# Joining three stages of an eight-layer transformer kernel: attention 1, routed feed forward 1 and retention

## The reference

```python
x = x + _L1_xattn_ref(_layernorm(x), ctx_1024, ctx_1024, mask, bias, ...)   # 16 heads of 8
x = x + _L1_ffn_ref(_layernorm(x), ...)
x = x + _L2_xattn_ref(_layernorm(x), ctx_1024, ctx_1024)                    # retention

# _L1_ffn_ref: 8 experts of inner width 64, 2 chosen, and a shared one of 128
logits = xf @ gate_w.T + lb_bias
scores = jax.nn.sigmoid(logits)
topw, topi = jax.lax.top_k(scores, K)
topw = topw / (topw.sum(-1, keepdims=True) + 1e-08)
for e in range(E):
    m = topi == e
    sel = m.any(axis=-1)
    wmean = (topw * m).sum() / jnp.maximum(m.sum(), 1)
    y = _mlp(xf, expert_gate_w[e], expert_up_w[e], expert_down_w[e])
    out = out + jnp.where(sel[:, None], y * wmean, 0)
out = out + _mlp(x, shared_gate_w, shared_up_w, shared_down_w)

# retention: q = xpos(Q), k = xpos(K): rotations of pairs; scores under a decay mask
scores = jnp.einsum('bhsd,bhtd->bhst', q, k) * D[None]
out = jnp.einsum('bhst,bhtd->bhsd', scores, v)
```

## Time and profile before

| | |
|---|---|
| median of 3 runs | 1600.39 us (1596.59 to 1604.29) |
| the profiled execution's own time | 1595.35 us, span 1593.5 us |
| TensorE, VectorE, ScalarE, GpSimd busy | 87%, 63%, 56%, 49% of the span |
| attention 1 | about 760 to 1006.35 us of the span |
| norm, gate and operands of feed forward 1 | 1006.4 to 1039.8 us |
| feed forward 1 | 1039.8 to 1099.8 us |
| norm and first rotation of retention | 1099.8 to 1120.35 us |
| retention | 1120.35 to 1180.8 us |
| feed forward 2, matmuls | about 1215 to 1311.9 us |

### The profile page before, as it was taken

How to read it: one execution, slowest core, us unless ns; L and a number is a source line. 1 busy time by engine, 2 the same in 40 slices (tenths; PEclk the granted TensorE clock), 3 DMA queues, 4 the chain that set the end, 5 groups by cost and what they waited for, 6 DMA issues and landing times.

```text
span 1593.5 us, 37007 instructions
## 1 busy us (share of the span) xinstructions
PE 1389.0 (87%) x14394; PEld 853.0 (54%) x14394; DVE 1006.3 (63%) x2452; ACT 887.8 (56%) x1456; POOL 774.9 (49%) x703
## 2 busy tenths in 40 slices
PE   5999999987899999998899898485776987999948
PEld 3666666655677777776344343243553553444425
DVE  5877777795634444447688888645664334666653
ACT  4877777765689999997444443121332223555512
POOL 5877777774579999897423231202301004334200
PEclk9999999998899999999799999698787996999968
DMA  8000000000112100010010110000000000000000
GB/s 260 8 8 2 8 8 8 2 15 28 31 32 90 56 26 26 26 47 28 4 60 31 38 50 1 1 0 27 2 3 1 1 7 4 8 8 5 1 1 27
DMA packets 26078, 39.53 MB, mean 25 GB/s; under 512 B 7060, under 2 KB 13112, under 8 KB 25432
## 3 DMA queue, kind: packets, MB, share of 16 engines
q1 hardware_dynamic: 25368, 35.58, 7.0%
q0 software_dynamic: 576, 2.10, 0.7%
HBM read 38.72 MB, written 1.05 MB: 25 GB/s over the span
## 4 chain that ended last, share of the span: by engine, by line
PE 67%; DVE 22%; issue 4%; ACT 4%; POOL 2%; DMA 1%; SPq 0%; POOLq 0%; DVEq 0%; ACTq 0%
PE bank L1660 10%; PE bank L1601 9%; PE bank L1927 5%; PE bank L681 5%; DVE sbuf L810 4%; PE bank L1913 4%; PE bank L1100 3%; PE bank L619 3%; DVE sbuf L827 2%; PE bank L1169 2%; PE bank L635 2%; DVE sbuf L332 2%; PE bank L1150 2%; PE bank L1120 2%; PE bank L1917 2%
## 5 line engine op out<-in xcount | busy, mean ns | idle before, releaser
L1611 ACT ACTIVATE sbuf<-bank,sbuf 128x512 f32<-128x512 f32 (+1 forms) x512 | 323.0, 684 | 36.7 <-PE bank L1601 24.7
L1631 POOL TENSOR_TENSOR sbuf<-sbuf 128x512 f16<-128x512 f32 x256 | 304.3, 1196 | 61.1 <-ACT sbuf L1611 59.9
L1660 PEld LDWEIGHTS bank<-sbuf 128*128 128x128 f16 x3072 | 194.9, 99 | 73.5 <-issue 14.5
L1660 PE MATMUL bank<-sbuf 128*128 128x128 f16 x3072 | 215.4, 220 | 12.4 <-DVEq L1748 6.3
L1601 PE MATMUL bank<-sbuf 128*128 128x512 f16 x768 | 209.1, 382 | 0.1
L810 DVE TENSOR_REDUCE sbuf<-bank 128x4 f32<-128x1024 f32 x128 | 156.2, 1221 | 75.6 <-PE bank L635 62.7
L312 POOL TENSOR_TENSOR sbuf<-sbuf 128x4 f32<-128x4 f32 (+2 forms) x21 | 28.3, 1349 | 348.1 <-DVE sbuf L307 348.1
L1063 POOL TENSOR_TENSOR sbuf<-sbuf 128x512 f16<-128x512 f32 x128 | 148.1, 1178 | 70.3 <-ACT sbuf L1279 70.2
L588 POOL TENSOR_TENSOR sbuf<-sbuf 128x512 f16<-128x512 f32 x64 | 66.6, 1040 | 234.9 <-ACT sbuf L740 234.9
L1743 DVE SCALAR_TENSOR_TENSOR sbuf<-bank,sbuf 128x128 f32<-128x128 f32 x256 | 71.7, 342 | 171.1 <-PE bank L1660 164.1
L681 PE MATMUL bank<-sbuf 128*32 128x256 f32 x2048 | 138.4, 389 | 1.6 <-ACT sbuf L760 1.6
(11 more groups left out here) (254 smaller groups left out, 2674.2 us busy)
## 6 DMA issues: line engine op xcount, KB each, us to landing
sbuf<-w SPq DMA_DIRECT2D x32, 256.0 KB, 2.9
sbuf<-bias_t SPq DMA_DIRECT2D x4, 1024.0 KB, 12.8
sbuf<-ctx_t SPq DMA_DIRECT2D x24, 128.0 KB, 3.5
sbuf<-bias_q POOLq DMA_DIRECT2D x4, 512.0 KB, 10.5
sbuf<-mask_t SPq DMA_DIRECT2D x8, 256.0 KB, 2.8
sbuf<-bias_t SPq DMA_DIRECT2D x8, 256.0 KB, 3.1
sbuf<-mask_q SPq DMA_DIRECT2D x8, 256.0 KB, 3.6
sbuf<-bias_q SPq DMA_DIRECT2D x8, 256.0 KB, 3.9
```

The costliest lines, as they stand in the source:

```text
L1611: last = act.activation(to, bank[u % 4][:, :], ACT.Gelu, bias=b1[u // U][:, u % FT0:u % FT0 + 1], scale=1 / SCALE)
L1631: g.tensor_tensor(hid16[1][:, u % BUFS, :], hid[:, u % 4, :], hid16[0][:, u % BUFS, :], ALU.subtract)\
L1660: last = pe.matmul(bank[4 + out_no % 2][:, j * P:(j + 1) * P], hid16[h][:, u % BUFS, j * P:(j + 1) * P], w2_16[p][:, w, f * D:(f + 1) * D] ...
```

## The change

`Gate` takes the place of `gate()` for feed forward 1 and works in two parts, tiles 0 to 11 and 12 to 15. `narrow_attention` gets two more arguments. Inside its loop VectorE takes the statistics of batch b-1 in unit 7 and scales batch b-2 in unit 1; GpSimd takes the power, splits the weights once (batch 1) and splits `xn_t` batch by batch; TensorE transposes batch b-2 in unit 2 and ScalarE copies it. In batch 7 the logits of the first part follow in unit 3 and their bias and negation in unit 4; after the loop come sigmoid, maxima and places of the first part between the last batch's steps.

`routed_feed_forward` takes the place of `feed_forward(1)`, unrolled. The four shared steps stand first, two of them before the gate; the projection down lags two steps. The mean goes into the fp16 spread table, whose high and low parts lie in different partitions (rows 0 to 7 and 32 to 39 of 64), so that one matmul makes the spread. Statistics and scaling of the next norm, the first two rotations of the queries (VectorE) and all rotations of keys (GpSimd) stand inside this stage; the context is loaded at its start, and retention's buffers lie apart from it. Feed forward 2 gets the same stacked spread. The diff, cut:

```diff
+        class Gate:
...
+            PARTS = ((0, 12), (12, TILES))
+            CHOSEN = 3
...
+            def logits(self, pe, h, to):
+                a, z = self.PARTS[h]
+                E = self.E
+                pe.wait_ge(nrm_xt, self.nm.ready(z // SB - 1))
+                for t in range(a, z):
+                    last = pe.matmul(to[:, (t - a) * E:(t - a + 1) * E], xn_t[:, t * P:(t + 1) * P], self.weights[:, 0:E],
+                                     start=True, stop=True)
+                last.then_inc(g_psum, 1)
...
+            def scores(self, v, h, src):
...
+            def exps(self, act, h):
...
+            def top(self, v, h):
...
+            def places(self, v, a, z):
...
+            def choose(self, v, h):
...
+            def turn(self, pe, k, to):
+                pe.wait_ge(g_ready, self.base["ready"] + (1 if k < self.CHOSEN else 2))
...
@@ -596,6 +725,17 @@
                 for b in range(B):
                     for k in range(QK):
                         split_(b, k)
+                    if after and b == 1:
+                        lead.weights(g)
+                    if after and b >= 2:
+                        after.power(g, b - 2, b - 1)
+                    if after and b >= 3:
+                        lead.halves(g, b - 3)
+                if after:
+                    lead.halves(g, B - 3)
+                    for b in (B - 2, B - 1):
+                        after.power(g, b, b + 1)
+                        lead.halves(g, b)
...
@@ -685,6 +825,8 @@
 
                 def out(b):
                     pe.wait_ge(s["normed"], b + 1)
+                    if after and b == B - 2:
+                        lead.gate.read(pe, 0)
...
+                    if after and b >= 2 and n == 2:
+                        after.turn(pe, b - 2, b - 1, bank[TR])
+                    if after and b >= 2 and n == 3:
+                        pe.wait_ge(nrm_xt, after.ready(b - 2))
...
+                    if after and b == B - 1 and n == 3:
+                        pe.wait_ge(x_done, x0 + B - 2)
+                        lead.gate.logits(pe, 0, bank[PR])
...
+                if after:
+                    after.turn(pe, B - 2, B - 1, bank[TR])
...
+                    if after and b >= 2 and n == 2:
+                        after.copy(act, b - 2, b - 1, bank[TR])
...
+                if after:
+                    lead.gate.exps(act, 0)
+                    after.copy(act, B - 2, B - 1, bank[TR])
...
+                    if after and b >= 2 and n == 1:
+                        after.scale(v, b - 2, b - 1)
                     if b and n == 2:
                         norm_out(b - 1)
                     if b and n == 6:
                         out(b - 1)
+                    if after and b and n == 7:
+                        v.wait_ge(x_done, x0 + b)
+                        after.stats(v, b - 1, b)
+                    if after and b == B - 1 and n == 4:
+                        lead.gate.scores(v, 0, bank[PR])
+                if after:
+                    after.scale(v, B - 2, B - 1)
+                    lead.gate.top(v, 0)
                 norm_out(B - 1)
+                if after:
+                    lead.gate.places(v, 0, 8)
                 out(B - 1)
+                if after:
+                    v.wait_ge(x_done, x0 + B)
+                    after.stats(v, B - 1, B)
+                    lead.gate.places(v, 8, 12)
+                    after.scale(v, B - 1, B)
...
+        def routed_feed_forward(layer, nm, after, ahead):
...
+            LAG = 2
+            RING = 4
...
+            inners = [(c, routed) for c in range(CHUNKS)] + [(c, t) for c in range(CHUNKS) for t in range(routed)]
+            downs = [(c, t) for c in range(CHUNKS) for t in [routed] + list(range(routed))]
...
+            def weights(g):
...
+            def halves(g, k):
...
+                def inner(m):
+                    c, t = inners[m]
+                    if m < CHUNKS:
+                        pe.wait_ge(s["x16"], 4 * c + 4)
+                    if m == 0:
+                        pe.wait_ge(s["w16"], WEIGHTS)
+                    if m >= 2:
+                        pe.wait_ge(s["hidden"], m - 1)
+                    if t < routed:
+                        gate.ready(pe, c)
+                        pe.wait_ge(s["spread"], 1)
...
+                    for b0, w16 in ((0, wg16), (2, wu16)):
+                        for k, (w, xk) in enumerate(PASSES):
+                            last = pe.matmul(bank[b0 + m % 2][:, :], w16[:, w, t * P:(t + 1) * P], x16[:, xk, cols],
+                                             start=k == 0, stop=k == 2)
+                    if t < routed:
+                        last = pe.matmul(bank[SPREADS[m % 2]][:, :], spread16[0:ROWS, t * P:(t + 1) * P],
+                                         gates16[0:ROWS, cols], start=True, stop=True)
+                    last.then_inc(s["inner"], 1)
...
+                for m in range(2):
+                    inner(m)
+                pe.wait_ge(nrm_xt, nm.ready(B - 2))
+                nm.turn(pe, B - 1, B, bank[TURNED])
+                gate.logits(pe, 1, bank[LOGITS])
+                for k in range(CHUNKS - 1):
+                    if k == 1:
+                        gate.read(pe, 1)
+                    if k >= 2:
+                        gate.ready(pe, k - 2)
+                    gate.turn(pe, k, bank[SPREADS[k % 2]])
+                gate.total(pe, bank[TOTALS])
+                gate.ready(pe, 1)
+                gate.turn(pe, CHUNKS - 1, bank[SPREADS[(CHUNKS - 1) % 2]])
+                for m in range(2, CHUNKS):
+                    inner(m)
+                d = 0
+                for m in range(CHUNKS, len(inners) + LAG):
+                    if m < len(inners):
+                        inner(m)
+                    while d < len(downs) and inner_no[downs[d]] <= m - LAG:
+                        down(d)
+                        d += 1
...
+                nm.copy(act, B - 1, B, bank[TURNED])
+                gate.exps(act, 1)
+                for k in range(CHUNKS):
+                    gate.turned(act, k)
+                    src = bank[SPREADS[k % 2]][0:E, :]
+                    cols = slice(k * CHUNK, (k + 1) * CHUNK)
+                    act.activation(gates16[HIGH, cols], src, ACT.Copy)
+                    act.activation(gates16[LOW, cols], src, ACT.Copy).then_inc(g_t, 1)
+                for m in range(len(inners)):
+                    act.wait_ge(s["inner"], m + 1)
+                    wait(act, s["hidden"], m - RING + 1)
+                    act.activation(acted[:, m % RING, :], bank[m % 2][:, :], ACT.Silu, scale=1 / SCALE).then_inc(s["acted"], 1)
...
+                def add(k):
+                    v.wait_ge(s["down"], (k + 1) * NT)
+                    xs = x[:, k * CT:(k + 1) * CT, :]
+                    v.tensor_tensor(xs, bank[DOWNS[k % 2]][:, :].rearrange("p (t d) -> p t d", d=D), xs, ALU.add)\
+                     .then_inc(x_done, 1)
+                    v.wait_ge(x_done, x0 + k + 1)
+                    after.stats(v, 2 * k, 2 * k + 2)
...
+                gate.choose(v, 0)
+                gate.scores(v, 1, bank[LOGITS])
+                gate.top(v, 1)
+                gate.places(v, 12, TILES)
+                gate.choose(v, 1)
+                gate.totals(v)
+                for m in range(2):
+                    hidden(m)
+                gate.mean(v, bank[TOTALS])
+                flat = spread[0:E, 0:routed, :].rearrange("p t c -> p (t c)")
+                c.step(v.tensor_scalar(spread16[HIGH], flat, wmean[0:E, 2:3], None, ALU.mult)).settle()
+                v.scalar_tensor_tensor(spread16[LOW], flat, wmean[0:E, 2:3], spread16[HIGH], ALU.mult, ALU.subtract)\
+                 .then_inc(s["spread"], 1)
+                for m in range(2, len(inners)):
+                    hidden(m)
+                    k = (m - CHUNKS - LAG - 1) // routed - 1
+                    if (m - CHUNKS - LAG - 1) % routed == 0 and k >= 0:
+                        add(k)
+                    if (m - CHUNKS - LAG - 1) % routed == 2 and k >= 0:
+                        after.scale(v, 2 * k, 2 * k + 2)
+                        ahead["rotate"](v, k)
+                after.scale(v, B - 4, B - 2)
+                ahead["rotate"](v, CHUNKS - 2)
+                add(CHUNKS - 1)
+                after.scale(v, B - 2, B)
+
+            def pool(g):
+                ahead["zeros"](g)
+                for k in range(CHUNKS):
+                    for b in (2 * k, 2 * k + 1):
+                        ahead["keys"](g, b)
+                    after.power(g, 2 * k, 2 * k + 2)
...
+                v.memset(spread16[0:ROWS], 0.0)
+                c.step(v.memset(gates16[0:ROWS], 0.0)).settle()
...
+                c.step(v.tensor_copy(spread16[HIGH], flat))
+                c.step(v.tensor_copy(gates16[HIGH], gt)).settle()
                 if layer == 1:
-                    last = v.tensor_tensor(spread16[0:E, 1, :], flat, spread16[0:E, 0, :], ALU.subtract)
```

(26 more changed lines are left out.)

241 lines of the change are left out of this document (208 added, 33 removed).

## The result

The changed kernel takes 1560.05 us (median of 4 runs, 1556.8 to 1563.14) beside 1600.27 us of the kernel before: a ratio of 0.9748, interval 0.9714 to 0.9782. The profiled execution took 1556.8 us (span 1555.0), where the sum had given 1556.3. The forecast of faster holds, and 1561 us is within the measurement. But the agreement to half a microsecond is luck: the attention loop cost 4.3 us less than its term, feed forward 2 gained 2.8 less than its own, and the first 810 us, for which the sum had nothing, were 2.3 us longer in this execution.

A forecast was written before the change was run, and what follows sets the result against it. TensorE and VectorE both nearly fill attention 1, TensorE bounds feed forward, and the gaps around it are serial. 7 + 1.4 - 37.5 - 2 - 8 = -39.1 from 1595.35 gives 1556.3, as a median 1561; range 1547 to 1581.

The forecast's parts named there:

- Part 1: Attention 1's loop: inserted statistics, scaling and transposes, plus logits in the last batch, cost +7 us (2 to 26).
- Part 2: Tail of attention: VectorE's norm of batch 6, sigmoid and 12 maxima before the last reciprocal cost +1.4 us (0 to 3).
- Part 3: From attention's last addition to retention's first mask: 119.5 us now, 82 after, a gain of 37.5 (bounds 73 and 90).
- together 10.5: After attention's last addition: batch 7's norm 2.3, the gate's first-part tables 2.7 and second part 5.5 us.
- 4.5, to 69: Feed forward 1: TensorE's stalls behind VectorE's additions, statistics, scaling and rotation, 4.5 us (1 to 9); last product at 69.
- Part 4: Retention: -2 us (0 to -5), as the second batch's transposes and the state are done when the first mask starts.
- Part 5: Feed forward 2: -8 us (-9 to -5), one spread pass of two saved per routed step, against one more copy.
- 32 x 0.53 / 2: Feed forward 2: 32 routed steps each lose half of the spread pair's 0.53 us, 8.5 us.
- The loop in full: Rival in attention 1: every insertion lands on the path, costing 26 us instead of 7; median 1580, chance 0.15.
- Feed forward 1 as VectorE's: Rival: VectorE's detours are all paid, none caught up, and the tail's scalings meet GpSimd; +10, median 1571, chance 0.12.
- The spread that gives nothing: Rival: 64 rows cost more than 16, or latency bounds feed forward 2; +8, median 1569, chance 0.07.
- The slower case: Attention loop: new work opens holes that drop TensorE to 1.2 GHz; all 48 units +82, median 1643, chance 0.06.

The follow-up runs named there:

- the spread alone: The kernel before with nothing but the stacked spread, in feed forward 1 and 2: ratio 0.9929, 1593.28 us beside 1604.50.
- the changed kernel's second profile: The changed kernel as it is, run again beside the version with both edits on one chip: 1559.58 us, ratio 0.9708; profiled execution 1564.73 us.

## Why the prediction was right, and where it was not

**Part 1 (+7) and Part 2 (+1.4): mechanism right, the loop mis-sized.** Measured +4.1 together in the first pair of profiles. The term was "five batches pay 0.85": they pay 0.17 each, 0.8 in all instead of 4.3. The transposes were charged at their full 0.45 and took 0.44, but half of such a piece is absorbed, as doubling it showed; the statistics were charged 0.3, and the two together cost 0.17; the scaling's 0.1 is 0, as doubling that showed. One reading behind the transposes was wrong too: the logits' 3.93 us in the earlier trace rows are not at the low clock (granted 0.90; at 0.50 the same logits took 6.64). The last batch was right in this pair: 1.6 for its start with the 24 logits, 1.5 to the last reciprocal, 0.2 behind it, 3.3 where 2 + 1.4 stood. But the last interval between reciprocals goes with the granted clock: with the new work it took 19.2 us at 1.00 (four profiles), 19.8 to 19.9 at 0.91 (four) and 22.1 at 0.77 (three), without it 17.0 at 1.00 (two) and 18.3 at 0.91. At the same clock the new work costs 1.5 to 2.2 us there. The level of 0.77 was seen only with it, in three profiles of eleven; whether the new work brings it about is not shown. With it, from the first reciprocal to the last addition the loop takes 203.6 us.

**Part 3 (-37.5): right by two errors that cancel.** Counted from the last addition:

| | predicted | measured |
|---|---|---|
| gate's sums ready | 10.5 | 13.4 |
| first product over | 15.2 | 18.6 |
| first routed step starts | 18.8 | 23.3 |
| stalls of TensorE behind VectorE | 4.5 | 0.6 |
| last product over | 69 | 69.5 |
| first mask | 82 | 82.0 |

The step that failed first is "together 10.5": it took VectorE's durations from a stretch in which GpSimd was still. The clears and the keys stood beside the gate and cost 2.5 us of these 2.9; without them it was 10.9. The shared steps 2 and 3 took 4.5 us and not 3.6: 2.3 each, near twice the 1.29 of the later ones, so mostly at the low level (granted clock 0.60 over the two). The step that failed in the other direction is "4.5, to 69" of stalls. By the same durations TensorE, from the first routed step on, would have led to a last product at 23.3 + 43.5 + 2.15 = 68.9; it was 69.5. I had given each step 1.6 us of air and let each detour use it alone. With two steps of lag the air of the following step counts too, and the three detours all but vanish; with one step they return, TensorE waits, and the stretch to the last product is 2.2 us longer. Hardly any of the 0.6 is a stall even then: the spread's 0.32 instead of 0.53/2 makes 0.9 in 16 steps, and the last product was over 2.4 us behind the last inner step, where 2.15 stood. The tail of 12.5 us for 13 was right term by term: addition and statistics 2.2, power 1.0, scaling 2.5, rotation 2.2 (for 2.95), once more 2.2 and 1.0, scaling 1.1.

**Part 4 (-2)** measured -2.5, and it is likely real: seven profiles with retention's code unchanged took 51.95 to 53.26 us at granted clocks of 0.94 to 0.97, against 54.66 and 54.95 in the two with the old joint at 0.94 and 0.95. The reason that was given for it was not tested. But one execution at 0.86 took 58.04, so a single profile could as well have shown the opposite.

**Part 5 (-8): the spread mis-sized, the logits not foreseen.** The matmuls to the last addition gained 9.2 us where -8.5 - 0.3 stood, but not for the reason given. A routed step took 2.06 for 2.27: one pass of two saved 0.21 us and not 0.265, 6.7 us over 32 steps and not 8.5. The step that failed is "32 x 0.53 / 2": the pair's 0.53 is not two equal halves. One of the six matmuls of 512 columns that a step of feed forward 1 has takes 1.29 / 6 = 0.21 over 128 rows; the same is what the second pass had cost, and 0.1 stayed with the first. The rest of the 9.2 is the clock at their start: the first 11.9 us of matmuls ran at 0.87, in the kernel before at 0.63. In the six profiles with short logits, where that stretch had 0.65 to 0.78, the matmuls gained 6.9 to 8.3. Against it the way to the first matmul grew by 4.0, not 0.7. Of these 2.7 are the logits at the low level, and the rest, 0.9 to 1.1 in the profiles with short logits, is the copy of 0.68 and the part of the clears that does not fit into the wait of 1.32. Short logits on both sides give 131.08 to 124.5, -6.6 on average: half of the miss of 2.8 us comes with the long logits, and the other half is mostly the spread's term.

**The rivals.** The loop in full fell: 0.61 us for the scaling, and 29.48 a batch. Its mechanism, VectorE beside GpSimd, was real, but it struck at the gate and not in the loop. Feed forward 1 as VectorE's fell too, but for the last 8.6 us before the end of the last product, where the chain is Silu's and VectorE's. The spread that gives nothing fell by the spread alone: 0.32 us for one matmul over 64 rows, 0.53 for two over 8 or 16. The slower case, TensorE's clock in the loop, did not come over whole batches: 1.00. It came in small in places I had not named: the last batch (0.77 in three profiles), the logits, and the starts behind a gap.

## What to carry to other kernels

Statistics, scaling and transposes of a norm can be strewn into a loop whose TensorE is idle 8% and whose VectorE 14% of the time, and cost a fraction of their length; behind the loop the same work put some 20 us on the path here. Before a sum takes VectorE's durations from a stretch in which GpSimd is still, look what the change puts on GpSimd beside them, and keep GpSimd still where VectorE is the chain. And ask of the work in a tail whether its reader really comes next: the scalings of four batches that retention's first mask doesn't read stood 6.7 us on the path. Last, compare two versions from an event on that both have, such as the first spread matmul here: from the stage's start one step of lag looked like no change, and from that event it is 1.3 us faster.

## What the hardware showed that I had not expected

- A VectorE operation of 0.18 us on 32 columns took 1.72 beside two GpSimd clears of 1.00 us each: it began 0.26 us behind the first and ended with the second, so it got no turn between them. In the changed kernel's second profile it was 1.65, and ended with the second too.
- The same code drew a different granted clock in different executions: 32 logits at 0.50 in 6.65 us or at 0.86 in 3.94; retention at 0.95 in 52.4 us or at 0.86 in 58.0.
- A GpSimd power of 2 columns took 0.70 us, of 4 columns 1.02, of 16 columns 2.91: eight small ones cost GpSimd 5.6 us where one large one took 2.9. Those of batches 0 to 5 are not on the chain of waits; that of batch 6 is, with its 0.70.
- One fp16 matmul of 512 columns over 64 rows added 0.32 us to a step, where two over 8 or 16 rows had added 0.53, and one of six over 128 rows takes 0.21. A pass less saved 0.21 in both feed forwards.
